# Three of the sixteen units of an attention set turned on VectorE instead of two, with other buffers and other orders around them

## The reference

```python
x = _layernorm(x + gru(relu((adj @ x) @ W_msg.T + b_msg), x))          # layer 0
x = _layernorm(x + D^-1/2 (adj + I) D^-1/2 @ (x @ W) + b)              # layer 1, D = row sums
# layer 2: masked attention, 4 heads of 32 features
q, k, v = x @ Wq + bq, x @ Wk + bk, x @ Wv + bv
attn = einsum('nhc,mhc->hnm', q, k) / sqrt(32);  neg = where(adj == 0, -inf, attn)
alpha = softmax(neg, axis=-1)
out = einsum('hnm,mhc->nhc', alpha, v);  x_r = x @ Ws + bs
beta = sigmoid(concat(out, x_r, out - x_r) @ Wb)
x = _layernorm(x + beta * x_r + (1 - beta) * out)
# layer 3: hyperbolic; xt is a row-wise function of x (Mobius product with a weight, a bias, a logarithm)
x = _layernorm(x + g(adj @ xt))                                        # g: row-wise
```

## Time and profile before

| | |
|---|---|
| median of three runs | 1786.05 us (1782.78 to 1787.19) |
| the profiled execution's own time | 1782.96 us |
| its span, first to last instruction | 1781.3 us |
| TensorE matmul busy | 1735.9 us, 97% |
| VectorE busy | 1228.6 us, 69% |
| ScalarE busy | 975.8 us, 55% |
| GpSimd busy | 895.6 us, 50% |
| mean granted TensorE clock | 0.993 |

### The profile page before, as it was taken

The page is one execution under the profiler, slowest core; times in us unless marked ns, Lnnn a source line. Parts: engine busy times, 40 slices in busy tenths (PEclk is TensorE's granted clock), DMA queues, the critical chain, the costliest instruction groups (busy, mean ns, idle before and its releaser), DMA issues.

```text
span 1781.3 us, 40266 instructions
## 1 busy us (share of the span) xinstructions
PE 1735.9 (97%) x15000; PEld 1131.3 (64%) x15000; DVE 1228.6 (69%) x2405; ACT 975.8 (55%) x1505; POOL 895.6 (50%) x849
## 2 busy tenths in 40 slices
PE   7999999999998999999999999999999999999996
PEld 3444444444444778877877887778778777644442
DVE  4777775222225889999999999999999999301322
ACT  0110111010103898999999999999999999411101
POOL 0212120112114755778878788788787896540211
PEclk9999999999998999999999999999999999999998
DMA  9866676899996544445445445454454543897981
GB/s 382 325 221 251 254 252 224 278 313 371 332 366 184 186 155 161 155 155 167 150 140 182 150 152 170 156 173 150 142 178 144 167 157 116 323 371 275 321 323 57
DMA packets 134029, 388.53 MB, mean 218 GB/s; under 512 B 15712, under 2 KB 66144, under 8 KB 109280
## 3 DMA queue, kind: packets, MB, share of 16 engines
q1 hardware_dynamic: 117792, 356.11, 57.6%
q10 hardware_dynamic: 13824, 22.75, 3.6%
q0 software_dynamic: 2240, 7.34, 1.6%
HBM read 333.19 MB, written 52.95 MB: 217 GB/s over the span
## 4 chain that ended last, share of the span: by engine, by line
PE 92%; DVE 4%; issue 1%; ACT 1%; DMA 1%; POOL 1%; DVEq 0%; ACTq 0%; POOLq 0%; SPq 0%
PE bank L592 35%; PE bank L742 23%; PE bank L763 14%; PE bank L701 13%; DVE arena L1281 2%; PE bank L580 1%; PE bank L655 1%; PE bank L614 1%; PE bank L613 1%; DMA arena<-x_dram 1%; PE bank L607 0%; PE bank L769 0%; PE bank L650 0%; PE bank L789 0%; PE bank L630 0%
## 5 line engine op out<-in xcount | busy, mean ns | idle before, releaser
L976 ACT ACTIVATE arena<-arena,small 128x2048 f32<-128x2048 f32 x256 | 516.2, 2016 | 2.8 <-DVE small L1281 2.8
L742 PE MATMUL bank<-ident,arena 128*128 128x128 f32 x3592 | 485.5, 278 | 4.4 <-ACT arena L976 2.6
L742 PEld LDWEIGHTS bank<-ident,arena 128*128 128x128 f32 x3592 | 398.1, 141 | 87.8 <-issue 41.9
L592 PE MATMUL bank<-arena,stat_s 128*128 128x512 f32 x1008 | 439.1, 592 | 2.1 <-issue 1.2
L988 ACT ACTIVATE arena<-bank 128x512 f32<-128x512 f32 x673 | 377.0, 604 | 66.2 <-PE bank L742 65.3
L701 PE MATMUL bank<-k,parts 128*128 128x512 f32 x1024 | 354.4, 436 | 10.6 <-DVE small L1281 10.6
L592 PEld LDWEIGHTS bank<-arena,stat_s 128*128 128x128 f32 x1008 | 189.2, 190 | 226.8 <-issue 225.4
L763 PE MATMUL bank<-arena,stat_x 128*32 128x128 f32 x8192 | 276.5, 276 | 0.0
L763 PEld LDWEIGHTS bank<-arena,stat_x 128*32 128x32 f32 x8192 | 208.1, 109 | 90.8 <-issue 81.5
L592 PE MATMUL bank<-arena,stat_x 128*128 128x512 f32 x512 | 228.3, 598 | 10.1 <-DMA arena<-adj_cols 7.8
L701 PEld LDWEIGHTS bank<-k,parts 128*128 128x128 f32 x1024 | 158.8, 192 | 29.6 <-DVE small L1281 24.5
(11 more groups left out here) (155 smaller groups left out, 1431.8 us busy)
## 6 DMA issues: line engine op xcount, KB each, us to landing
arena<-adj_cols SPq DMA_DIRECT2D x190, 1024.0 KB, 6.4
stat_s<-adj SPq DMA_DIRECT2D x85, 512.0 KB, 4.8
group_dram<-stat_s SPq DMA_DIRECT2D x63, 512.0 KB, 2.9
arena<-group_dram SPq DMA_DIRECT2D x252, 128.0 KB, 2.8
arena<-adj SPq DMA_DIRECT2D x43, 512.0 KB, 4.6
parts<-q_dram SPq DMA_DIRECT2D x128, 64.0 KB, 2.4
k<-k_dram POOLq DMA_DIRECT2D x28, 256.0 KB, 9.5
x_dram<-arena ACTq DMA_DIRECT2D x16, 256.0 KB, 3.7
```

The lines of the kernel that those rows point to most:

```text
L592: mm_ = pe.matmul(bank[:, to, :], stat[:, jt, :], ring[:, s, j, :], start=(jt == 0), stop=(jt == TILES - 1))
L742: last = pe.transpose(bank[:, b_, h * P:(h + 1) * P], cols[:, st % SETS, h, u * P:(u + 1) * P], ident[:, :])
L976: act.activation(cols[:, s_, h, :], cols[:, s_, h, :], ACT.Exp, bias=shift[:, t % 2, 1, i:i + 1], scale=-1.0, accum_out=blocksum[:, t % 2, ...
```

## The change

1. Units 13, 14 and 15 of a set form the group; 13 units are turned by TensorE. VectorE transposes the three blocks at places 1, 2 and 6. The group is 768 KB. The last set has three units left to TensorE instead of two.
2. The copies are divided anew: VectorE has 23 a chunk, ScalarE 81. The places of the exponents move. The 8 slots are given out over the units that TensorE turns (`slot_of`, `used_before`).
3. The attending is in three batches of a set: at place 4 the last four units of the set before, at place 8 units 0 to 5, at place 14 units 6 to 11. At the end of the stage four units are left.
4. The group's landing place moves to `stat_s`, and so there are two `adj_in` buffers instead of three, and the blocks of `adj` are loaded seven ahead. In SyncE's order the mask load of a set moves behind the group's store. `load_group` waits for the use of the set before instead of a unit of its own set.
5. `xt` of chunks 0 to 5 is spilled, each stored by GpSimd's own queue right after its computation. Chunks 0, 1 and 5 are loaded before the first four ring slots of layer 3, chunks 2, 3 and 4 behind them.
6. Two post steps move by two places (113 to 115, 119 to 121).

```diff
-ATTEND_BATCH = 4
-ATTEND_LAG = 8
-BLOCK_TURN_AT = {14: 3, 15: 5}
-GROUPS = ((14, 15),)
-VECTOR_PLACES = (6,)
...
+ATTENDS = {4: (-4, -3, -2, -1), 8: (0, 1, 2, 3, 4, 5), 14: (6, 7, 8, 9, 10, 11)}
+BLOCK_TURN_AT = {13: 1, 14: 2, 15: 6}
+GROUPS = ((13, 14, 15),)
+VECTOR_PLACES = ()
+VECTOR_ALSO = (5, 6, 7, 19, 25, 27, 38, 54, 58, 59, 66, 69, 82, 86, 87, 91, 92, 97, 99, 103, 119, 121, 123)
+EXP_MOVED = {9: 6, 13: 12, 17: 18, 21: 22, 25: 26, 29: 27, 33: 34, 37: 38, 41: 40, 45: 44, 49: 52, 53: 55, 57: 58, 61: 60, 65: 67, 69: 70, 73: 72, 77: 76, 81: 82, 89: 86, 93: 91, 97: 99, 101: 102, 105: 103, 109: 108, 117: 119, 125: 123}
...
-MASK_AHEAD = 8
-MASKS = 3
-SPILLED = (2, 3, 4, 5)
+MASK_AHEAD = 7
+MASKS = 2
+SPILLED = (0, 1, 2, 3, 4, 5)
+FIRST_XT = (0, 1, 5)
+OTHER_XT = (2, 3, 4)
...
+def attended_at(c, k):
+    u = k % UPS
+    return [k - u + a for a in ATTENDS.get(u, ())]
+
+def slot_of(k):
+    return (PE_UNITS + LAST_UNITS).index(k) % TURNED
...
-        group_slots = arena[:, RING + 10 * CHUNK:RING + 12 * CHUNK]
-        adj_in = (arena[:, RING + 4 * CHUNK:RING + 6 * CHUNK], spilled[:, 0:2 * CHUNK], spilled[:, 2 * CHUNK:4 * CHUNK])
+        adj_in = (arena[:, RING + 4 * CHUNK:RING + 6 * CHUNK], spilled[:, 0:2 * CHUNK])
+        group_slots = spilled[:, 2 * CHUNK:5 * CHUNK]
+        blocks = [stat_s[:, TILES - 3 * TPC:TILES, :].rearrange("p t f -> p (t f)")]
...
-                if g * UPS + GROUPS[i][-1] >= TURNED:
-                    sp.wait_ge(unit_used, g * UPS + GROUPS[i][-1] - TURNED + 1)
+                if g > 0:
+                    sp.wait_ge(unit_used, (g - 1) * UPS + GROUPS[i][-1] + 1)
...
-                    load_mask_ahead(c, 2 * st + 0)
                     if g < GROUP_SETS:
                         store_group(g, 0)
-                    if st == 0 and c - 2 in SPILLED:
-                        store_xt(c - 2)
+                    load_mask_ahead(c, 2 * st - 1 if g == 0 else 2 * st)
                     if g < GROUP_SETS:
                         load_group(g, 0)
...
+                    load_mask_ahead(c, 2 * st + 1)
...
                 if c == CHUNKS - 1:
+                    load_first_xt()
                     load_ring(2, 0, True, range(4))
+                    load_other_xt()
                 load_residuals(c)
...
-                    if (k - ATTEND_LAG) % ATTEND_BATCH == 0:
-                        for a in range(k - ATTEND_LAG, k - ATTEND_LAG + ATTEND_BATCH):
...
+                    for a in attended_at(c, k):
...
-                        weights = turned[k % TURNED][:, h * P:(h + 1) * P]
+                        weights = turned[slot_of(k)][:, h * P:(h + 1) * P]
...
+            pe.wait_ge(first_xt_in, 16 * len(FIRST_XT))
...
+                    if c in SPILLED:
+                        pool.wait_ge(att_pool, AG(c, "xt"))
+                        pool.dma_start(xt_dram[c - SPILLED[0], :, :], mx_g).then_inc(xt_out, 16)
```

More of the change, by code:

```diff
@@ L122 @@
 LAST_UNITS = [k for k in range(UPC - UPS, UPC) if k % UPS in BLOCK_TURN_AT]
+LAST_BY_VECTOR, LAST_BY_SCALAR = LAST_UNITS[0::2], LAST_UNITS[1::2]
 def is_block_turned(c, k):
@@ L214, in build_program @@
     xt_dram = nc.dram_tensor("xt_dram", [len(SPILLED), P, CHUNK], F32)
-    group_dram = nc.dram_tensor("group_dram", [len(GROUPS), P, 2 * CHUNK], F32)
+    group_dram = nc.dram_tensor("group_dram", [len(GROUPS), P, 3 * CHUNK], F32)
     k4_dram = nc.dram_tensor("k4_dram", [CHUNKS, 2, H, C, CHUNK], F32)
@@ L287, in build_program @@
         cols = arena[:, 0:RING].rearrange("p (s h n) -> p s h n", s=2, h=H)
+        spilled = stat_s[:, SPILLED[0] * TPC:(SPILLED[-1] + 1) * TPC, :].rearrange("p t f -> p (t f)")
         turned = [stages[i] for i in (0, 1, 6, 7, 2, 3, 10, 11)]
[L289 to L293 removed]
+        adj_in = (arena[:, RING + 4 * CHUNK:RING + 6 * CHUNK], spilled[:, 0:2 * CHUNK])
+        group_slots = spilled[:, 2 * CHUNK:5 * CHUNK]
+        blocks = [stat_s[:, TILES - 3 * TPC:TILES, :].rearrange("p t f -> p (t f)")]
         maskbias = [half_[:, i * BLOCK:(i + 1) * BLOCK] for half_ in
@@ L305, in slots_of @@
         def slots_of(i):
-            first, n = GROUPS[i][0] % TURNED - 6, len(GROUPS[i])
-            return group_slots[:, first * CHUNK:(first + n) * CHUNK]
+            return group_slots[:, 0:len(GROUPS[i]) * CHUNK]
         def tiles(ap):
@@ L483, in attention_loads, with load_xt, load_first_xt @@
                 if c == CHUNKS - 1:
+                    load_first_xt()
                     load_ring(2, 0, True, range(4))
+                    load_other_xt()
                 load_residuals(c)
[L487 to L491, removed]
+            def load_xt(chunks, landed):
+                for i in chunks:
+                    sp.dma_start(spilled[:, i * CHUNK:(i + 1) * CHUNK], xt_dram[i, :, :]).then_inc(landed, 16)
+            def load_first_xt():
                 sp.wait_ge(bias_ready, CHUNKS * COLS)
@@ L494, in load_xt, with load_other_xt @@
                     sp.wait_ge(group_out[i], 16 * GROUP_SETS)
-                for i in range(len(SPILLED)):
-                    sp.wait_ge(xt_out, 16 * (i + 1))
-                    sp.dma_start(spilled[:, i * CHUNK:(i + 1) * CHUNK], xt_dram[i, :, :]).then_inc(xt_in_place, 16)
+                sp.wait_ge(xt_out, 16 * len(SPILLED))
+                load_xt(FIRST_XT, first_xt_in)
+            def load_other_xt():
+                sp.wait_ge(unit_used, GROUP_SETS * UPS)
+                load_xt(OTHER_XT, xt_in_place)
             def load_residuals(c):
@@ L541, in _ @@
                              q_parts[:, i, :].bitcast(F32)).then_inc(gcn_q_out, 16)
-            load_mask(0, 5)
+            load_mask(0, 4)
             sp.wait_ge(gcn_dve, CV(last, "root"))
             sp.dma_start(root_dram[:, last * CHUNK:CHUNKS * CHUNK], root_out).then_inc(gcn_root_out, 16)
-            for m in range(6, MASK_AHEAD):
+            for m in range(5, MASK_AHEAD - 1):
                 load_mask(0, m)
@@ L548, in _ @@
                 attention_loads(c)
-            load_xt()
             load_ring(2, 0, True, range(4, SLOTS))
@@ L721, in wait_for_copy @@
             def wait_for_copy(c, k):
[L722 to L726, removed]
+                if k in LAST_BY_VECTOR:
+                    pe.wait_ge(unit_copied_dve, CHUNKS * len(BY_VECTOR) + LAST_BY_VECTOR.index(k) + 1)
+                elif k in LAST_BY_SCALAR:
+                    pe.wait_ge(unit_copied_act, CHUNKS * len(BY_SCALAR) + LAST_BY_SCALAR.index(k) + 1)
                 elif k in BY_VECTOR:
@@ L797, in attention @@
                             scores(*ahead, first and k < UPS)
-                    if (k - ATTEND_LAG) % ATTEND_BATCH == 0:
-                        for a in range(k - ATTEND_LAG, k - ATTEND_LAG + ATTEND_BATCH):
[L800 to L803, removed]
+                    for a in attended_at(c, k):
+                        if a >= 0:
+                            attend(c, a, first)
+                        elif not first:
+                            attend(c - 1, UPC + a, False)
                     if not is_block_turned(c, k):
@@ L815, in attention @@
                 if last_chunk:
-                    for a in range(UPC - ATTEND_LAG, UPC):
+                    for a in range(UPC - 4, UPC):
                         attend(c, a, first)
@@ L849, in _ @@
             HELD_BANKS = (0, 4, 5)
-            product(2, 0, {0: [final_out], SPILLED[0] - 1: [lambda: pe.wait_ge(xt_in_place, 16 * len(SPILLED))], 5: [lambda: pe.wait_ge(att_pool, AG(last - 1, "xt"))],
+            pe.wait_ge(first_xt_in, 16 * len(FIRST_XT))
+            product(2, 0, {0: [final_out], 1: [lambda: pe.wait_ge(xt_in_place, 16 * len(OTHER_XT))], 5: [lambda: pe.wait_ge(att_pool, AG(last - 1, "xt"))],
                            6: [lambda: turn_x3(last, 2)]}, slots=range(SLOTS - 1))
@@ L981, in copy_unit @@
                 if not (first and k < TURNED):
[L982 to L988, removed]
+                    act.wait_ge(unit_used, used_before(c, k))
+                elif k >= TURNED - 2:
+                    act.wait_ge(gcn_x2_out, 16 * CHUNKS)
+                elif k >= TURNED - 4:
+                    act.wait_ge(gcn_k_out, 32 * CHUNKS)
+                act.activation(turned[slot_of(k)], bank[:, unit_bank(k), :],
                                ACT.Copy).then_inc(unit_copied_act, 1)
@@ L1049, in attention @@
                         block_weights(c, k // UPT)
-                    if k in BY_SCALAR or (last_chunk and k == LAST_UNITS[1]):
+                    if k in BY_SCALAR or (last_chunk and k in LAST_BY_SCALAR):
                         copy_unit(c, k, first)
@@ L1289, in copy_unit @@
                 if not (first and k < TURNED):
[L1290 to L1296, removed]
+                    dve.wait_ge(unit_used, used_before(c, k))
+                elif k >= TURNED - 2:
+                    dve.wait_ge(gcn_x2_out, 16 * CHUNKS)
+                elif k >= TURNED - 4:
+                    dve.wait_ge(gcn_k_out, 32 * CHUNKS)
```

(5 more changed lines are left out.)

19 lines of the change are left out of this document (10 added, 9 removed).

## The result

The changed kernel took 1806.55 us (median of four runs, 1803.5 to 1809.65) against 1786.07: the ratio is 1.012 [1.010, 1.014]. It is slower, outside the forecast's range of 1755 to 1790. The profiled execution took 1805.16 us, span 1803.4.

What follows compares the result with a forecast made beforehand. TensorE was taken to set the attention's pace, VectorE following closely and becoming the pace after the change. Terms -14.4 - 3 - 2 + 1 = -18.4 took the profiled 1782.96 to 1764.6, or 1768 against the median; range 1755 to 1790.

Steps and rivals of the forecast that it cites:

- Two buffers for adj, seven ahead: Mask loads of the attention: about 6 us free in a buffer's cycle, later start loads covered; cost zero.
- GpSimd's stores: Six feature stores issued by GpSimd instead of four by SyncE: 21 us free a chunk, cost zero.
- TensorE, 13.97 us a set: TensorE's steps in an attention set: 13.97 us instead of 14.57, saving 4.8 us a chunk.
- VectorE, +2.0 a chunk, least 116.4: Attention: 8 more transposes, 5 fewer copies, +2.0 us; VectorE becomes the pace, middle chunk least 116.4, expected 117.5.
- the first chunk: First attention chunk: VectorE less busy there, so TensorE's saving counts more; -3 us, between 2.1 and 4.8.
- ScalarE, zero, at worst 2 us a chunk: Attention: three fewer copies; cover for copies of units 5 and 11 just fits; zero, at worst 2 us a chunk.
- The group's round trip, slack 1.6: Group's store and load, 16.3 us at most against use at 17.9: slack 1.6 us, cost zero.
- Layer 3: Start of layer 3: three features loaded ahead of the ring, three behind; zero, at worst 2.8 us.
- the group comes late: Rival: round trip over 10.6 us, TensorE stands at place 4 of each set; 1830 us, chance 0.07.
- VectorE is the pace already: Rival, every set: VectorE's 6.6 us idle are needed gaps, its 2.0 us a chunk add +14; 1800, chance 0.10.

Runs made afterwards that it cites:

- the earlier blend: The changed kernel with GpSimd's blend of `y` at slot 8 instead of 9, ahead of a bias: 1776.35 us, ratio to the kernel before 0.9943.

## Why the prediction was wrong

The miss is 38.6 us. Moving one step of GpSimd gives back 30.2 of it. What was wrong is a mechanism: two terms were put at nothing that act through GpSimd.

*"Two buffers for adj, seven ahead ... Zero"* is the step that failed. It took a buffer's cycle as load plus bias, 8.4 us in a set of 14.6, and called the rest free. But a load starts when SyncE's queue comes to it, not when the buffer is free, and in that queue stand the wait for VectorE's last transpose and the wait for the landing of the group's store (us in total, times, longest):

```profile
SPq L463 <- DVE stat_s L1322: 297.8, 63, 9.7
...
SPq L474 <- DMA group_dram<-stat_s: 190.9, 63, 4.6
```

The trace showed 6.9 us between a free buffer and its load. Before, the queue was held no less, 195.2 us for the transposes and 351.3 for TensorE's use of a unit, but with the third buffer GpSimd waited for `adj` by 1.3 us only. The step did name who stands behind a blocked load; it did not ask what the load stands behind. Shown: two buffers alone, in the kernel before, cost 22 us, and two thirds of it came back when two steps of GpSimd stood earlier.

*"GpSimd's stores ... Zero"* was wrong twice. "21 us free a chunk" is a mean; in the 31.6 us from the features to `y` GpSimd was busy for 29.0, the rest in gaps of 0.25 us and less between its steps, and its last result was due 0.3 us after it came. Lateness there is paid (VectorE's 4.3 us), and none of the rivals had this place: a hidden engine that is just in time. And the store itself is a gain of 14.4 us where GpSimd is in time: it leaves SyncE's queue free between the group's store and its load, and TensorE's waits for the group are 9.8 us fewer.

*TensorE, 13.97 us a set:* right in kind. 63 units fewer are turned, and with GpSimd in time TensorE is busy for 115.7 us of a middle chunk, 119.4 before: 3.7 less instead of 4.8.

*VectorE, +2.0 a chunk, least 116.4:* right in kind. With GpSimd in time a middle chunk has 114.6 us of VectorE work on average (113.1 before, 115.3 forecast). The middle chunks of that run average 118.95 us instead of 117.5. These 1.5 us, six times, and the 3 us that the first chunk did not gain are most of the 13.4 us between its profiled execution (1778.0) and the one forecast (1764.6).

*ScalarE, zero, at worst 2 us a chunk:* nearer to the worst. TensorE's turning waited 11.2 us for ScalarE's copies (L1006); with the earlier blend 12.1, or 1.5 a chunk. That this is the missing 1.5 is argued only: moving two copies gained nothing. VectorE is full in one set of a chunk, ScalarE nearly so two sets later; what the rest waits for stays open.

*The group's round trip, slack 1.6:* it held in the changed kernel (1.9 us of waiting in all), and it is thinner than it was said: with the 4.1 and 3.8 us measured, the same sum leaves 0.5. Each of the four runs that put another transfer ahead of the group's store or load made TensorE wait for the group, 15 to 20 us in all.

*Layer 3:* as forecast; the first chunk gained nothing instead of 3.

*The rivals:* "the group comes late" did not happen here, but does in four experiments. "VectorE is the pace already" came nearest in time (1800) and names the wrong engine; that it came near is luck. The Trainium skill (Perfetto Trace Analysis, "Identifying the Most-Contended Engine") ranks engines by their share of busy time. GpSimd stands behind VectorE and ScalarE in the earlier trace rows (98.3 us against 113.3 and 112.1), and yet its late result cost the changed kernel 30.2 us; here the measurement decides against that order.

## What to carry to other kernels

Before a buffer is taken away, follow the queue that fills it: what does the load stand behind, and when does that come free? An engine at 80% can be the next bound; look for the place where its result arrives just when it is asked for, and count the reserve there, not in the mean. Where a slower version appears, first try the late step one place earlier: here that turned a loss of 20 us into a gain of about 9.

## What was not expected of the hardware

After TensorE's wait of 3.2 us, its next score pair took 1.22 us and 48 attending matmuls 2.79 us; a few microseconds before, in the rows above, the same 48 took 1.52. The granted clock there, in the columns of the earlier trace rows:

```profile
1360.00:1366.00 6.00, 6.00 (x58) 4.52 (x59) 3.84 (x12) 0.24 (x2) 5.29 (x4) 0.50 0.48 131
```

That is the lower of the two levels (1.2 and 2.4 GHz); in the long set as a whole it was 0.83, in those of the five other chunks 0.91. So the stall of 3.2 us cost about 5, which is the excess of that set (20.3 instead of 15.0).
